# Second-layer dense tiles and mu products placed in the slots of layer 3's FFN tiles, last norms placed in the experts loop

## The chip, the cores and the metric

The kernel runs on one core of one Trainium2 chip. The metric is the device time in microseconds (us) of one execution. Three executions of the kernel before gave a median of 2058.72 us (2057.43 to 2061.12). Everything is float32.

The engines are TensorE (PE; PEld is its weight load), VectorE (DVE), ScalarE (ACT), GpSimd (POOL) and SyncE (SP, which only issues DMAs here). Each runs its own program in order and waits on semaphores for the others.

## The reference, cut to what matters

3125 nodes with 256 features, 53125 edges sorted by destination, in two halves with weights of their own.

```python
xn = _layernorm(x)
# graph part: two layers
h = xn + res * conv(xn, rel1, W_in1, W_out1, W_loop1, b1)
h = h  + res * conv(h,  rel2, W_in2, W_out2, W_loop2, b2)
g = h @ mu_w + mu_b
#   conv: m = x[src] * rel[type];  first half @ W_in, second half @ W_out
#         agg = segment_sum(m / deg[dst]);  tanh(agg + x @ W_loop + b)
# mix part: four layers (0 to 3) of linear attention and FFN on xn
x = x + g + mix(xn)
# last part: norm, gates over 4 experts (softmax, top 2, softmax again),
# shared MLP 256-256-128-256, experts 256-128-64-256
y = _layernorm(x);  x = x + shared(y) + sum(topw * expert(y))
```

## The kernel before, in words

Rows are worked on in 25 tiles (NT) of 125 nodes (T), five groups (NG) of five tiles (GT). The mix part runs layer by layer; a layer is a `joint` (end of attention's context) and five `iteration`s, one per group. In an iteration each tile's FFN is an up product (`Feed.up`, L2398: 16 matmuls of 125 columns in two halves), ScalarE's gelu, and a down product (`Feed.down`, L2413: 8 matmuls of 256 columns); beside them stand attention (`attend`) and turned rows (`turn`) of the next group. A float32 matmul is two instructions in the trace.

The graph layers run beside the mix layers as **edge steps** of 128 edges. GpSimd gathers a step's source rows (L837) and, in the first graph layer, its relation rows (L817). VectorE multiplies two steps at a time (a unit) with the relation rows and makes the one-hot rows of the destinations (`Edges.unit`, L959 and L968). TensorE sums them per destination (`Edges.unit` on TensorE, L2294), and VectorE adds every eight steps into `acc` (L947). The buffer holds 16 gathered steps, the one-hot ring 8. How many steps stand where is written out by hand (STEPS_GROUP, `marks`, and `upto(...)` between the FFN products); the same marks are used on VectorE and TensorE. The second graph layer has 416 steps: 92 in group 4 of layer 2, 36 in the joint of layer 3, and 60, 60, 60, 60, 48 in the groups of layer 3.

Once all steps of a graph layer are summed, the **dense** part takes each tile: VectorE scales the sums (L1483), TensorE turns sums and rows (L499) and multiplies them with the two weights (L2711), VectorE adds the bias (L1556), ScalarE takes the tanh (L2161), VectorE adds it to the rows (L1534). For the first graph layer this stands before group 4 of layer 2, for the second one (`dense(1)`) it stands behind all of layer 3. `dense_and_last` adds to the second one, some steps behind each tile, the mu product (`mu_beside`, L2782), its addition to the rows (`z_sum`, L1586, with the statistics in L1588), the last norm per group of five tiles (L1665 and `inv_sqrt`, then L1675), the turned norm rows and the gate logits (L2798, L1574). One piece more than tiles is needed because one tile holds edges of both halves. Gates are computed for 15 tiles at once and then for 10 (GATES). `general` is a path for unsorted edges, taken only if a flag made in the prologue is set; it stands behind the last edge step of each graph layer.

Last comes the **experts loop**: per tile `shared_1` (L2748), `turn_experts`, `experts_1` (L2757), `layer_2` (L2865, L2870) and `layer_3` (L2888, L2890) on TensorE, and `gated_rows` (L1828, L1831), `add_experts` (L1845) and `add_biases` (L1836, L1839) on VectorE. GpSimd adds x into the rows by DMA (`add_x`, L805) and loads the last weights (L874 to L888).

Of the kernel before, what the change touches and what calls it, by code (L numbers as in the profile page):

```python
# [14 lines left out]
P = 128  # L15
# [28 lines left out]
def build(nc, io, out):  # L44
# [37 lines left out]
    PD_INDICES, PD_ROWS, PD_FALLS, PD_KEYS = 3, 10, 21, 43  # L82
# [7 lines left out]
    LAST_LOADS = 11 + NX  # L90

# [9 lines left out]
    with ExitStack() as ctx:  # L101
# [98 lines left out]
        norm = qm[:, 0:NT]  # L200
# [36 lines left out]
        split_node_i, split_node = scratch(T, 1).bitcast(I32), scratch(T, 1)  # L237
# [5 lines left out]
        first, tile_of, base, place, bad = (scratch(SCH, 4) for _ in range(5))  # L243
# [16 lines left out]
        g_columns = hot[:, 1:1 + KC, :].rearrange("p s t -> p (s t)")  # L260
# [3 lines left out]
        gateb = key_tab[0:T, 0:NX]  # L264
        lmask = key_tab[0:T, NX:NX + NX * NX].rearrange("p (a b) -> p a b", b=NX)
# [12 lines left out]
        beat, beat2 = (last_buf(NT, NX, NX) for _ in range(2))  # L278
        assert last_at[0] <= GT * (D + AW)
        sb1p, sb2p, eb1p = b1p[:, 0:KC], b1p[:, KC:KC + 1], b1p[:, KC + 1:KC + 1 + NX]  # L280
# [248 lines left out]
        H2, MU, ZT = 2, 3, 11  # L529
        LG = ZT + 1  # L530
        DRAIN = LG + 2

# [3 lines left out]
        def dense_and_last(tile, beside):  # L536
            for t in range(NT + DRAIN):
                if t < NT:
                    tile(t)
                beside(t)  # L540

        def piece(g, t):

            return g * NB + t + 1


        GATES = (slice(0, 3 * GT), slice(3 * GT, NT))

        GATE_STEPS = (3, 4, 6)

        ps_logit = [ps_seg[1]] * 3 + [ps_kv, ps_dn]
        assert NG == len(ps_logit)
# [44 lines left out]
        for name, cols in (("mu", KC * D), ("sW1", KC * D), ("sW2", KC * P), ("sW3", D), ("eW1", NX * KC * P),  # L597
                           ("eW2", NX * EH2), ("eW3", KC * D), ("gW", KC * NX)):
            offs[name] = (at, at + cols)
            at += cols  # L600
        assert at <= 2 * KC * FF

        def last_w(name, c):
            a, b = offs[name]
            return wff[:, a:b].rearrange("p (c n) -> p c n", c=c)

        mu_w, sW1, sW2, gW = (last_w(n, KC) for n in ("mu", "sW1", "sW2", "gW"))
# [88 lines left out]
        def _(sp):  # L696
# [9 lines left out]
            sp.dma_start(split_node_i, io["dst"][HALF - 1:HALF].partition_broadcast(T)).then_inc(s_split, 16)  # L706
            load_ln1(sp, 0)

            def dense_rows(g):
# [19 lines left out]
                for t in range((NT - AHEAD) // AHEAD * AHEAD, NT):  # L729
                    if g == 0:  # L730
                        store_h1(t, t)
# [2190 lines left out]
```

## Time and profile before

| what | value |
|---|---|
| median of 3 executions | 2058.72 us |
| profiled execution | 2060.31 us |
| its span in the trace | 2058.6 us |
| TensorE busy | 1880.9 us (91%) |
| VectorE busy | 1259.6 us (61%) |
| ScalarE busy | 674.2 us (33%) |
| GpSimd busy | 1339.0 us (65%) |
| granted TensorE clock, mean | 0.979 |

The rows that follow are of three kinds. A row of a table of stretches gives busy time (and count) of each engine in a stretch. A row of a timeline gives the start of a run of like instructions, how long the run lasted, engine, line, operation, output and inputs, and in brackets how long the engine had been idle before it and what released it. The spacing of starts is the cadence of the engine, while the durations of overlapping matmuls add up to more. A row of groups gives busy time, mean duration of one and the idle time ahead of them. L-numbers are lines of the kernel before.

### The profile page before, as it was taken

The numbers are of one execution on the slowest core, as the hardware profiler recorded it, in microseconds if no ns is written. First come the engines' busy times: TensorE is split into PE (matmuls) and PEld (weight loads), VectorE is DVE, ScalarE is ACT, GpSimd is POOL, SyncE is SP. The second block draws the span as 40 slices with busy tenths as digits, with TensorE's granted clock in tenths as the row PEclk, the third lists the DMA queues.
The fourth block names the chain that finished last, engine by engine and source line by source line (L and its number), as shares of the span: only waits on it lengthen the run. The fifth ranks groups of instructions, "written<-read, shape, count | busy, mean of one in ns | idle before, by whom it ended". The sixth has DMA issues, their size and how long they took to land.

```text
span 2058.6 us, 32009 instructions
## 1 busy us (share of the span) xinstructions
PE 1880.9 (91%) x10496; PEld 1566.3 (76%) x10496; DVE 1259.6 (61%) x3295; ACT 674.2 (33%) x1858; POOL 1339.0 (65%) x1342
## 2 busy tenths in 40 slices
PE   3989999998999999989999897788988999899999
PEld 1558888886788888678888785566877778778998
DVE  6775576556657556665655654487656556456666
ACT  5432344343234334422433341122112112133443
POOL 5777777777777777777777227777777777720000
PEclk9999999999999999999999999899999999999999
DMA  8677666667766666776667337766666666650001
GB/s 240 186 247 217 199 188 193 204 198 239 229 197 190 196 202 197 239 227 196 192 205 215 94 114 262 222 200 213 199 192 201 194 199 198 148 106 14 14 16 36
DMA packets 191812, 371.61 MB, mean 181 GB/s; under 512 B 36589, under 2 KB 123035, under 8 KB 191656
## 3 DMA queue, kind: packets, MB, share of 16 engines
q0 software_dynamic: 78624, 225.58, 38.1%
q1 hardware_dynamic: 92986, 128.48, 19.1%
q10 hardware_dynamic: 20046, 15.57, 2.7%
q8 instruction: 86, 1.41, 0.3%
q14 instruction: 70, 0.57, 0.1%
HBM read 305.39 MB, written 64.95 MB: 180 GB/s over the span
## 4 chain that ended last, share of the span: by engine, by line
PE 58%; POOL 16%; DVE 10%; issue 7%; DMA 6%; ACT 2%; DVEq 1%; ACTq 0%; SPq 0%
POOL xg L837 13%; PE ps_down L2417 11%; PE ps_hid L2408 10%; PE ps_seg L2294 10%; PE ps_kv L2327 4%; DMA xg<-h_rows,idx_tab 4%; POOL rg L817 3%; PE ps_x L2372 2%; PE ps_hid L2757 2%; DVE xg L968 2%; PE ps_kv L2711 2%; PE ps_down L2711 2%; PE ps_x L499 2%; PE ps_hid L499 2%; PE ps_hid L2347 1%
## 5 line engine op out<-in xcount | busy, mean ns | idle before, releaser
L2294 PE MATMUL ps_seg<-xg,hot 128*125 128x257 f32 x1664 | 444.4, 395 | 85.6 <-DVE xg L968 84.8
L837 POOL DMA_INDIRECT xg<-h_rows,idx_tab x416 | 431.9, 1038 | 134.3 <-issue 116.4
L837 POOL DMA_INDIRECT xg<-xn_rows,idx_tab x416 | 431.3, 1037 | 127.8 <-issue 121.9
L817 POOL DMA_INDIRECT rg<-relation_rows,idx_tab x416 | 425.4, 1023 | 129.5 <-issue 129.2
L2294 PEld LDWEIGHTS ps_seg<-xg,hot 128*125 128x125 f32 x1664 | 293.9, 191 | 161.9 <-DVE xg L968 87.6
L2408 PEld LDWEIGHTS ps_hid<-hT,wff 128*128 128x128 f32 x3200 | 384.1, 192 | 15.8 <-issue 6.8
L2408 PE MATMUL ps_hid<-hT,wff 128*128 128x125 f32 x3200 | 387.9, 275 | 1.6 <-ACT gT L1950 0.9
L968 DVE TENSOR_TENSOR xg<-xg,rg 128x512 f32<-128x512 f32 x416 | 286.0, 688 | 157.2 <-DMA xg<-h_rows,idx_tab 129.5
L1950 ACT ACTIVATE gT<-ps_hid,b1p 128x125 f32<-128x125 f32 x800 | 225.9, 366 | 471.0 <-PE ps_hid L2408 470.8
L2417 PE MATMUL ps_down<-wff,gT 128*125 128x256 f32 x1600 | 368.0, 384 | 0.0
L2417 PEld LDWEIGHTS ps_down<-wff,gT 128*125 128x125 f32 x1600 | 299.7, 191 | 43.6
L959 DVE TENSOR_TENSOR hot<-iota_t,key_tab 128x250 f32<-128x250 f32 x416 | 170.9, 411 | 9.3 <-issue 5.3
L1134 DVE TENSOR_TENSOR xres<-xres,ps_down 125x256 f32<-125x256 f32 x100 | 40.1, 418 | 125.0 <-PE ps_down L2417 124.5
L2327 PE MATMUL ps_kv<-wqkv,hTa 128*125 128x512 f32 x240 | 113.7, 596 | 0.0
L1865 ACT ACTIVATE kx<-ps_kv 125x256 f32<-125x256 f32 x74 | 28.4, 384 | 249.3 <-PE ps_kv L2327 238.0
L1940 ACT ACTIVATE hT<-ps_x,ln2p 128x250 f32<-128x250 f32 (+1 forms) x120 | 56.0, 522 | 158.9 <-PE ps_x L499 158.5
L947 DVE SCALAR_TENSOR_TENSOR acc<-ps_seg,in_tile,acc 125x257 f32 x208 | 99.6, 479 | 4.2 <-PE ps_seg L2294 3.6
L1086 DVE TENSOR_TENSOR xres<-xres,ps_x 125x256 f32<-125x256 f32 x80 | 30.8, 418 | 113.3 <-PE ps_x L2372 113.3
L2372 PE MATMUL ps_x<-cwo,qT_all 128*125 128x256 f32 x320 | 77.7, 382 | 0.0
L2327 PEld LDWEIGHTS ps_kv<-wqkv,hTa 128*125 128x125 f32 x240 | 45.2, 189 | 33.8 <-issue 29.4
L2372 PEld LDWEIGHTS ps_x<-cwo,qT_all 128*125 128x125 f32 x320 | 60.4, 189 | 9.6
L1894 ACT ACTIVATE hTa<-ps_x,ln1p 128x125 f32<-128x125 f32 x120 | 48.3, 462 | 42.2 <-PE ps_x L499 42.2
(362 smaller groups left out, 2391.4 us busy)
## 6 DMA issues: line engine op xcount, KB each, us to landing
second_relation_rows<-rg SPq DMA_DIRECT2D x104, 512.0 KB, 4.0
rg<-second_relation_rows SPq DMA_DIRECT2D x104, 512.0 KB, 3.9
wff<-L_mix_W ACTq DMA_DIRECT2D x8, 1024.0 KB, 7.0
rg<-relation_rows,idx_tab POOLq DMA_INDIRECT x416, 3.5
xg<-xn_rows,idx_tab POOLq DMA_INDIRECT x416, 3.3
xg<-h_rows,idx_tab POOLq DMA_INDIRECT x416, 3.7
h_rows<-rg SPq DMA_DIRECT2D x25, 112.0 KB
xres<-x POOLq DMA_DIRECT2D x5, 560.0 KB, 8.6
```

Of the source, the lines that this page charges most:

```text
L499: ins = pe.transpose(dst[:, c * T:(c + 1) * T], rows[:, c * P:(c + 1) * P], ident[0:T, 0:T])
L817: pool.indirect_dma_start(rg[:, k, :], None, rel_d, bass.IndirectOffsetOnAxis(ap=idx_tab[:, step, 1:2], axis=0))\
L837: pool.indirect_dma_start(xg[:, k, 0:D], None, rows, bass.IndirectOffsetOnAxis(ap=idx_tab[:, step, 0:1], axis=0))\
L947: dve.scalar_tensor_tensor(a, ps_seg[w % 2][0:T, 0:AW], in_tile[:, ds(w, 1), m], a, ALU.mult, ALU.add).then_inc(s_acc, 1)
L959: dve.tensor_tensor(hot[:, hs:hs + UNIT, :], iota_t[:, :].unsqueeze(1).broadcast_to([EP, UNIT, T]), key_tab[:, at:at + UNIT].unsqueeze(2). ...
L968: dve.tensor_tensor(m, m, r, ALU.mult).then_inc(s_msg, 1)
L1950: ins = act.activation(gT[:, j % 2, ff, :], ps_hid[hf][:, f * T:(f + 1) * T], ACT.Gelu, bias=b1p[:, ff:ff + 1])
L2294: ins = pe.matmul(ps_seg[u // UW % 2][0:T, 0:AW], hot[:, s % HOTS, :], xg[:, s % RING, :], start=s % WIN == 0, stop=s % WIN == WIN - 1)
L2327: ins = pe.matmul(ps_kv[0:T, :], hTa[:, j % 2, c, :], wqkv[:, c, 0:2 * D], start=c == 0, stop=c == KC - 1)
L2372: ins = pe.matmul(ps_b[j % 2][0:T, :], q[:, c * T:(c + 1) * T], cwo[:, c, :], start=c == 0, stop=c == KC - 1)
L2408: ins = pe.matmul(ps_hid[hf][:, f * T:(f + 1) * T], w1[:, c, ff * P:(ff + 1) * P], hT[:, j, c, :], start=c == 0, stop=c == KC - 1)
L2417: ins = pe.matmul(ps_down[j % 2][0:T, :], gT[:, j % 2, f, :], w2[:, f, :], start=f == 0, stop=f == FC - 1)
```

## The change

The second graph layer's dense tiles no longer wait for the last edge. Destinations are sorted, so a tile's sums are complete once the edge windows that reach it are added (`windows_of`). A piece k of the 26 (25 tiles and the split tile's extra product as piece 11) is carried through two slots, and an iteration of layer 3 has ten slots between its FFN products: `aside(0)` to `aside(9)`. Rows of the first layer's result come tile by tile over ScalarE's DMA queue into `qrow`. The mu products follow two pieces later. What is left of pieces 24 and 25 stands behind the last group.

The last norm of group 0 is made in the last iteration, those of groups 1 to 4 in the experts loop (tile by tile of the loop: statistics and norm; rows; turned rows; logits; gates). Gates are made for five tiles at a time. The branch to the general path of the second layer moves ahead of layer 3's groups; its flag is also set if an edge comes earlier than the new order allows, or if the split lies outside tiles 11 to 13. Loads of the last weights move from GpSimd's to SyncE's queue. GpSimd's adds of x wait for the group's mu sums too. Nothing changes in the numbers of edge steps and their marks.

```diff
 # VectorE
-            def iteration(lay, gi, upto, one, early, sums_done, joint_rest):
+            def iteration(lay, gi, upto, one, early, sums_done, joint_rest, aside):
...
                 upto(m["up0"])
+                if not is_first(gi):
+                    aside(-1)
...
                 upto(m["up1"])
+                aside(0)
                 upto(m["down0"])
+                aside(1)
                 b.add_ffn(0)
...
                 early()
+                aside(8)
+                if (lay, gi) == (L - 1, NG - 1):
+                    last_norm(0)
                 b.add_ffn(3)
...
+            def dense_beside(s):
+                k = s // 2
+                if s % 2 == 0:
+                    rows_updated(k - 1)
+                    mu_added(k - 2)
+                    sums_scaled(k + 1)
                 else:
-                    dense_and_last(dense_tile, lambda t: z_beside(t, update))
+                    product_biased(k)
...
+                    if (lay, gi) == (L - 1, 0):
+                        general(1)
+                        self_split.read()
+                        sums_scaled(0)
+                        gate_order()
...
-            dense(1)
+            behind = NG * (2 * GT)
+            dense_beside(behind - 1)
+            dense_beside(behind)
+            logits(0)
+            shift_logits(0)
+            dense_beside(behind + 1)
+            dense_beside(behind + 2)
+            softmax(0)
+            top_two(0)
+            dense_beside(behind + 4)
+            gates(0)
...
             for s in range(1, NT + 2):
+                gi, j = last_part(s)
                 if s <= NT:
                     gated_rows(s - 1)
                 if s > 1:
                     add_experts(s - 2)
                 if s <= NT:
                     add_biases(s - 1)
-                if s in GATE_STEPS:
-                    gate_steps[GATE_STEPS.index(s) + 1](1)
+                if gi < NG:
+                    if j == 0:
+                        last_stats(gi)
+                    if j == 1:
+                        last_rows(gi)
+                    if j == 3:
+                        logits(gi)
+                        shift_logits(gi)
+                    if j == 4:
+                        softmax(gi)
+                        top_two(gi)
+                        gates(gi)
 # ScalarE
+            def dense_beside(s):
+                k = s // 2
+                if s % 2 == 0:
+                    loop_tanhs(k - 1)
+                    sums_turned(k)
+                else:
+                    rows_turned(k - 1)
...
                 b.gelu(0)
+                aside(0)
                 b.gelu(1)
...
+                aside(1)
+                aside(2)
...
+                aside(3)
+                aside(4)
                 b.gelu(3)
...
+                aside(5)
+                aside(6)
                 b.gelu(4)
+                aside(7)
 # TensorE
                 up(0, None)
+                aside(0)
                 up(1, "up0")
...
+                aside(1)
                 b.down(0)
...
                     n.attend(1)
+                aside(2)
...
+                aside(3)
...
                 b.down(1)
                 upto(m["down1"])
+                aside(4)
...
+                aside(5)
...
                 b.down(2)
                 upto(m["down2"])
+                aside(6)
                 up(4, "down2")
+                aside(7)
...
                 b.down(3)
                 upto(m["down3"])
+                aside(8)
...
                 b.down(4)
                 upto(m["ctx"])
+                aside(9)
...
+            def dense_beside(s, split_tile):
+                k = s // 2
+                if s % 2 == 0:
+                    turn_sums(k)
+                    mu_product(k - 2)
                 else:
-                    dense_and_last(dense_tile, mu_beside)
+                    sum_product(k, split_tile)
+                    turn_rows(k - 1)
...
+            behind = NG * (2 * GT)
+            turn_last(0)
+            turn_last(1)
+            dense_beside(behind, split_tile)
+            for j in range(2, GT):
+                turn_last(j)
+            dense_beside(behind + 1, split_tile)
+            last_logits(0)
+            pe.wait_ge(s_ew, 16 * LAST_LOADS)
+            pe.wait_ge(s_gel, L * (2 * NT) + 2)
+            shared_1(0)
+            dense_beside(behind + 2, split_tile)
+            experts_1(0)
+            dense_beside(behind + 3, split_tile)
+            dense_beside(behind + 4, split_tile)
             for s in range(1, NT + 2):
...
                 if s < NT:
                     shared_1(s)
+                if gi < NG and j == 3:
+                    last_logits(gi)
+                turn(0)
                 if s > 1:
                     turn_experts(s - 2)
+                turn(1)
 # GpSimd
             def add_x(gi):
                 pool.wait_ge(s_xr, NG * L + gi + 1)
+                pool.wait_ge(s_emz, (gi + 1) * GT)
...
+                    if g == GL - 1 and step == at_group[L - 1, 0] - STEPS2:
+                        hold(pool, s_seg, g * UNITS + step // UNIT + 1)
+                        general(1)
```

## Rows read from the trace of the kernel before

**Rows 1.** table of stretches: us from to, length, busy (count) per engine, clock, DMA share, GB/s
```profile
1415.00:1495.00 80.00, 72.29 (x394) 62.08 (x393) 49.92 (x128) 15.61 (x47) 62.33 (x59) 0.96 0.63 200
...
1797.00:1916.00 119.00, 106.93 (x630) 92.53 (x629) 70.14 (x250) 43.91 (x110) 16.00 (x21) 0.94 0.28 58
...
1916.00:2058.00 142.00, 138.01 (x1079) 132.66 (x1079) 95.08 (x228) 55.69 (x196) 0.00 (x0) 0.99 0.08 24
```

**Rows 2.** the page's groups: the gathers of the second graph layer
```profile
L837 POOL DMA_INDIRECT xg<-h_rows,idx_tab x416 | 431.9, 1038 | 134.3 <-issue 116.4
```

**Rows 3.** who waited for whom, TensorE, 1415 to 1797 us: total, times, longest
```profile
PE ps_seg L2294 <- DVE xg L968: 34.9, 46, 3.1
```

**Rows 4.** timeline of TensorE, layer 3, group 0 and the last down product
```profile
1415.40 1.94 PE L2408 MATMUL ps_hid<-hT,wff 128*128 128x125 f32 x16
...
1472.03 3.62 PE L2417 MATMUL ps_down<-wff,gT 128*125 128x256 f32 x16
1475.48 1.03 PE L2294 MATMUL ps_seg<-xg,hot 128*125 128x257 f32 x4
1476.35 1.94 PE L2408 MATMUL ps_hid<-hT,wff 128*128 128x125 f32 x16
1478.13 1.90 PE L2294 MATMUL ps_seg<-xg,hot 128*125 128x257 f32 x8
...
1495.50 1.95 PE L2408 MATMUL ps_hid<-hT,wff 128*128 128x125 f32 x16
...
1793.49 3.62 PE L2417 MATMUL ps_down<-wff,gT 128*125 128x256 f32 x16
```

**Rows 5.** timeline of TensorE, dense tiles and logits behind layer 3
```profile
1819.26 0.38 PE L499 MATMUL ps_hid<-ident,xg 125*128 125x125 f32 x2
...
1819.69 1.89 PE L2711 MATMUL ps_kv<-wqkv,gT 128*125 x8
1821.42 0.38 PE L499 MATMUL ps_x<-ident,acc 125*128 125x125 f32 x2
1821.64 1.03 PE L2782 MATMUL ps_seg<-wff,hT 128*125 128x256 f32 x4
1822.50 0.38 PE L499 MATMUL ps_hid<-ident,xg 125*128 125x125 f32 x2
...
1850.08 0.50 PE L2798 MATMUL ps_seg<-wff,qT_all 128*125 128x4 f32 x4
```

**Rows 6.** timeline of VectorE, experts loop: gated rows and experts added
```profile
1965.48 0.42 DVE L1828 TENSOR_TENSOR xh<-ps_x,bo_b 125x256 f32<-125x256 f32 x1 [1.32 <-PE ps_x L2870]
...
1966.83 0.42 DVE L1845 TENSOR_TENSOR xres<-xres,ps_kv 125x256 f32<-125x256 f32 x1 [0.47 <-PE ps_kv L2890]
```

**Rows 7.** timeline of ScalarE behind layer 3; table loads from 1797 us on
```profile
1812.43 0.42 ACT L2161 ACTIVATE acc<-acc 125x256 f32<-125x256 f32 x1 [2.78 <-DVE acc L1556]
...
L2210 ACT ACT_TABLE_LOAD x1 | 1.3, 1283 | 0.0
```

**Rows 8.** timeline of VectorE in the prologue: the first multiplied messages
```profile
51.08 0.69 DVE L968 TENSOR_TENSOR xg<-xg,rg 128x512 f32<-128x512 f32 x1 [3.59 <-DMA xg<-xn_rows,idx_tab]
```

**Rows 9.** timeline of TensorE, experts loop: starts of the shared product
```profile
1916.38 2.05 PE L2748 MATMUL ps_hid<-qT_all,wff 128*128 128x125 f32 x8
...
1961.05 1.05 PE L2748 MATMUL ps_hid<-qT_all,wff 128*128 128x125 f32 x8
...
1966.56 1.05 PE L2748 MATMUL ps_hid<-qT_all,wff 128*128 128x125 f32 x8
```

**Rows 10.** timeline of VectorE: last norm of five tiles, gates of 15 tiles
```profile
1905.65 0.45 DVE L1665 BATCH_NORM_AGGREGATE mv<-stat 125x2 f32<-125x6 f32 x5
...
1908.15 1.70 DVE L1675 TENSOR_SCALAR acc<-xres,mv,rstd 125x256 f32<-125x256 f32 x5
...
1914.39 0.22 DVE L1607 TENSOR_REDUCE kx<-kx 125x15 f32<-125x60 f32 x1 [4.16 <-ACT kx L2210]
...
1918.94 0.18 DVE L1574 TENSOR_TENSOR kx<-ps_kv,key_tab 125x20 f32<-125x20 f32 x1
```

More of the change, by code:

```diff
@@ L90, in build, with due_node, windows_of, tile_of_piece @@
     LAST_LOADS = 11 + NX
+    REST = 11
+    SPLITS = range(REST, REST + 3)
+    DUE_STEP, DUE_NODE, DUE_PITCH = 51 * WIN, (NT - 1) * T + 4, 125.0 / 2048.0
+    def due_node(edge):
+        return DUE_NODE + (edge - DUE_STEP * EP) * DUE_PITCH
+    def windows_of(t):
+        for w in range(STEPS2 // WIN):
+            chunk, step = divmod(w * WIN, SCH)
+            if due_node(CHUNKS[chunk][0] + step * EP) >= (t + 1) * T:
+                return w
+        return STEPS2 // WIN
+    def tile_of_piece(k):
+        return k if k < REST else -1 if k == REST else k - 1
+    def has_tile(k):
+        return 0 <= k < NB and k != REST
     xn_d = nc.dram_tensor("xn_rows", [N, D], F32, kind="Internal").ap()
@@ L242, in build @@
         spans = scratch(SCH, 4 * EP).rearrange("p (c t) -> p c t", c=4)
-        first, tile_of, base, place, bad = (scratch(SCH, 4) for _ in range(5))
+        first, tile_of, base, place, bad, due = (scratch(SCH, 4) for _ in range(6))
         reached = scratch(SCH, 4 * (NT - 1)).rearrange("p (c t) -> p c t", c=4)
@@ L1438, in general @@
             def general(g):
[L1440 removed]
+                row, other, onehot, turned = G_ROWS[g]
+                ps_turned, ps_product, ps_summed = ps_general[g]
+                if g == 0:
+                    hold(dve, s_acc, 2 * WINS + 3)
+                else:
+                    hold(dve, s_cw, L)
                 with dve.If(dve.value_load(unsorted_i[0:1, 0:1], min_val=0, max_val=1) == 1):
@@ new lines, in dense, with sums_scaled @@
+                update(NT - 1)
+                hold(dve, s_hn, NT)
+                dve.wait_ge(s_azero, NB)
+            def sums_scaled(k):
+                if not 0 <= k < NB:
+                    return
+                t = tile_of_piece(k)
+                need = windows_of(SPLITS[-1] if t < 0 else t)
+                assert edges.added() >= need, (k, edges.added(), need)
+                dve.wait_ge(s_acc, WINS * 2 + edges.adds + 3)
+                edges.scaled += 1
+                if k > 1:
+                    dve.wait_ge(s_dtr, SLOTS + NB + k - 1)
+                at, factor = (self_split.rest, norm[:, ds(self_split.rest_norm, 1)]) if t < 0 else                     (self_split.tile_sums(t), norm[:, t:t + 1])
+                dve.tensor_scalar(sums2[k % 2], at_tile(acc, at)[:, 0:D], factor, None, ALU.mult).then_inc(s_sc, 1)
@@ L1732, in _ @@
             p(dve.tensor_reduce(bad, spans, AX, ALU.add))
+            p(dve.tensor_tensor(due, due, first, ALU.is_gt))
+            p.wait()
+            p(dve.tensor_tensor(bad, bad, due, ALU.add))
             p.wait()
```

742 lines of the change are left out of this document (423 added, 319 removed).

## The prediction

> **What bounds the kernel now.** I read the table of stretches first [rows 1]. In the first group of layer 3 all engines work together: TensorE is shown busy 72.3 of 80 us, GpSimd 62.3, VectorE 49.9, ScalarE 15.6, and the same pattern holds for the next three groups. From 1797 us on GpSimd has nothing more to gather, and TensorE alone sets the pace: 119 us up to the experts loop, then 142 us of that loop. So 261 of 2058.6 us run with GpSimd idle and, before them, TensorE shares its time with a gather stream that it often waits for.
>
> Who waits for whom in layer 3 comes second. GpSimd issues one gather per edge step: 1038 ns busy and 134.3/416 = 0.32 us before each, nearly all of it put down to issue, not to a wait [rows 2]. A step therefore costs 1.36 us, a group of 60 steps 81.7 us, and the group measured 1495.50 - 1415.40 = 80.1 us [rows 4]. TensorE waits 34.9 us for multiplied messages, in 46 pieces [rows 3]; nothing else holds it there. Layer 3 is gather-bound.
>
> What TensorE really needs I take from starts, not from durations, since matmuls overlap [rows 4]. The down product of a tile takes 1475.48 - 1472.03 = 3.45 us, two edge steps 0.87 (0.435 each), half an up product 1.78 (3.56 per tile). The attention product of a tile is two matmuls of 256 columns like those of mu, 0.86, and a pair of transposes 0.22 [rows 5]. A tile is 8.1 us, five are 40.5, 60 steps are 26.1: 66.6 us of work in an 80 us group. The last group (48 steps, no next group to attend) needs 35.1 + 20.9 = 56.0. Together 322 us of work lie between 1415.40 and the end of the last down product at 1793.49 + 3.5 = 1797 us, 381.6 us. TensorE has 59 us of holes there.
>
> **The change part by part.**
>
> *Dense tiles and mu move into layer 3.* A tile of the second layer's dense work is, start to start, 1822.50 - 1819.26 = 3.24 us of TensorE: sums and rows turned 0.43, four matmuls 1.73, the new rows turned 0.22, mu 0.86 [rows 5]. Over five groups the 50 slots hold 24 tiles' turns and products (24 x 2.16 = 51.8), the split tile's extra product (1.1), 23 turns back (5.0) and 22 mu products (18.9): 76.8 us. TensorE's need becomes 322 + 76.8 = 399 us against 381.6 measured, so the bound changes hands: an inner group asks 66.6 + 15.4 = 82 us of TensorE, 80 to 82 of GpSimd. Two streams that are this close don't fill every hole; I add 6 us for holes that stay (1 to 2 us a group instead of 13.6). The lower end is 17 us (TensorE never waits), the upper is 77 (no hole used); I take 17 + 6 = 23, since 34.9 us of waits are scattered over 46 places and the slots come every 8 us. VectorE gets about 1.6 us more per tile (scale, bias, update, mu added, 0.35 to 0.48 each by like operations [rows 6]), 8 us a group on top of 46 to 50 of 80: covered. ScalarE gets two copies and a tanh, some 1.3 us a tile on top of 15.6 us a group: covered. Which waits are late next: the product needs ScalarE's copy from one slot earlier, and a 3.5 to 7 us FFN product lies between; the turn back needs VectorE's update, issued just after the same edge units that TensorE has yet to multiply, with 1.7 us of the sum product ahead of it. I cost these at nothing; the rival below prices them.
>
> *Tanh among gelus.* The row shows Tanh in the tail, after layer 3's gelus, with no table load between, and the only load after 1797 us is that of the gates' Exp, 1283 ns [rows 7]. So nothing is added. The Trainium skill ("ScalarE: Activation LUTs", section on table sets) lists tanh with exp and with sigmoid, gelu as the anchor of a set of its own, and advises batching by set; by that rule each tile would switch twice. The trace disagrees with that reading, but it is a rival below.
>
> *General path and index work ahead of layer 3.* It isn't taken: the destinations are sorted and the new due condition adds nothing to the count for these inputs (the closest edge lies 119 nodes above its bound, from the input arrays). What remains is a value load and a branch on three engines, four memsets and a read of the split numbers on VectorE, ahead of group 0, and a branch inside GpSimd's gather stream, which delays every later gather. No row shows it alone. Ends 0 and 8 us; I take 3. The dozen small VectorE operations in the prologue (under 0.2 us each, 2 us) hide behind the first gather, for which VectorE sat idle 3.59 us [rows 8]: 0.
>
> *Loads.* The last weights go from GpSimd's queue to SyncE's and start some 20 steps before the end, mu's weights and the h1 rows to ScalarE's. They land long before their readers; the experts' first tile has more than 20 us. The adds of x still follow the last gather and land while the last edges are summed. Nothing. Earlier loads could slow the last gathers: under 3 us, in the range.
>
> *The drain.* Before, 1916.38 - 1793.49 = 122.9 us pass from the last edge product (the last down product starts there) to the loop's first shared product [rows 4, 9]. After, what is left there, from that same point: VectorE's last adds and slot 8, 2.8; norm of group 0: statistics 1.8 and then 1908.15 - 1905.65 = 2.5 [rows 10]; first row 0.4: 7.8 (TensorE's down product and tile 24's products run beside it). Two FFN adds, bias of tile 24, mu of tile 23: 11.5. Turned rows, tile 25's product: 14.4. Five pairs of logits at 0.4 (0.50 shown for one [rows 5]): 16.4. Shared product, mu, experts' product: 20.4. ScalarE's relus and the copy for the last mu product, which TensorE waits for: 23.8. So 24 us, ends 20 and 34, and 99 us are saved.
>
> *The experts loop.* It runs at 1966.56 - 1961.05 = 5.51 us a tile on TensorE, with VectorE idle 1.32 and 0.46 us [rows 6, 9]: slack 1.78 a tile. New per group of five tiles on TensorE: 5 x (0.22 + 0.36) = 2.9. New on VectorE: 4.3 (statistics, norm) in one tile, 1.7 (rows) in the next, 0.6 and 3.6 (gates; 1918.94 - 1914.39 = 4.55 for 15 tiles, less for 5) later [rows 10]. The 3.6 and the next group's 4.3 stand in tiles that follow each other: 7.9 + 1.7 against 3 x 1.78 of slack and 1.05 us by which the gated rows were early leave TensorE waiting 3.3. So 6.2 a group, four groups: 25 us. The ends are 12 (VectorE wholly hidden) and 40 (all 10.2 us of VectorE in series).
>
> *Sum.* 23 + 3 - 99 + 25 = -48 us. The profiled execution took 2060.31 us (span 2058.6 and 1.7 around it), so 2012.3; it lay 1.6 above the median of 2058.72, so 2010.7. I forecast 2011.
>
> **The rivals.**
> 1. *Hand-over stalls* (the slower side): each slot puts TensorE in order behind a step of ScalarE or VectorE. If VectorE stands at a wait of its own when its part is due (it waits for gathers and for FFN products there now), TensorE idles and the gathers with it. Over 50 slots it decides from 48/50 = 0.96 us each; at 1.2 us the time is 2011 + 60 = 2071. For it: VectorE's idle share. Against it: the slots of the three programs stand behind the same edge marks. 0.06. At 0.5 us each it is 2036: 0.12.
> 2. *The loop hides VectorE's work*: 12 in place of 25, 1998. The gates and rows are short and TensorE's own extra work gives VectorE time. 0.17.
> 3. *The loop takes it in series*: 40 in place of 25, 2026. 0.12.
> 4. *Table loads*: 24 tiles x 2 x 1283 ns [rows 7] = 62 us, on the path 2073; against it stands the tanh row. 0.01. The skill page's rule named above is this mechanism; its own figure with the drain (2.66 us) would make it estimated at 128 us.
> 5. *Taken general path*, or the order of the slots not as the text says: 0.01, far slower.
>
> **How the numbers follow.** Forecast 0.51. The range must take in rivals 2 and 3 and the layer term's spread: the low end is 2011 - 13 (rival 2) - 6 (no holes left) - 2 = 1990; the high end 2011 + 25 (half-microsecond stalls) + 4 = 2040. A measurement here can tell about 0.2%, 4 us. Faster 0.90, within 0.2% 0.03 (the far flank of rival 1), slower 0.07.
>
> **What would show it.** Right: groups of layer 3 at 82 to 85 us with TensorE's waits for messages below 15 us; last edge product at 1815 to 1825; 22 to 30 us to the loop; loop tiles of 5.5 us with one stop of 2 to 4 us in five, before the turn of gated rows. Wrong: groups at 90 us with waits for ScalarE's copies or VectorE's updates (rival 1); a table load per tile (4); the last edge still at 1795 (TensorE's need overrated); loop tiles even at 6.1 (2) or at 7.5 (3).

## The result

| | changed kernel | kernel before |
|---|---|---|
| median of 15 runs, us | 2050.37 (2043.79 to 2054.97) | 2063.2 (2057.43 to 2076.59) |
| ratio, 95% interval | 0.9927 (0.9912 to 0.9942) | |
| profiled execution, us | 2053.1 (span 2051.4) | 2060.31 (span 2058.6) |

The change makes the kernel faster by 0.73% (0.58 to 0.88%), about 13 to 15 us. The forecast was 48 us less, 2011, with a range that ended at 2040: right in the sign, wrong in the size, and the measured 2050.37 lies outside the range. In the comparisons below, a run that took over 1.5% more than the fastest run of its kernel is left out.

The table of stretches of the changed kernel: us from to, length, busy us (instructions) of PE, PEld, DVE, ACT and POOL, granted clock as a share of full speed, DMA share, GB/s. The first five are the groups of layer 3, the sixth is the drain, the last the experts loop.

```profile
1424.00:1504.00 80.00, 74.08 (x423) 65.69 (x424) 53.20 (x143) 19.55 (x56) 61.71 (x61) 0.98 0.71 217
1504.00:1591.00 87.00, 85.00 (x483) 75.98 (x483) 52.60 (x132) 20.76 (x62) 64.12 (x60) 0.98 0.61 187
1591.00:1677.00 86.00, 85.74 (x496) 76.38 (x495) 52.49 (x133) 21.16 (x62) 63.60 (x62) 1.00 0.63 193
1677.00:1764.00 87.00, 85.00 (x483) 75.84 (x482) 52.24 (x131) 20.87 (x62) 67.57 (x62) 0.98 0.61 191
1764.00:1838.00 74.00, 74.00 (x438) 66.45 (x437) 39.32 (x94) 18.95 (x57) 46.55 (x44) 1.00 0.70 165
1838.00:1857.00 19.00, 15.11 (x98) 12.90 (x97) 9.66 (x43) 7.33 (x20) 0.00 (x0) 1.00 0.01 1
1857.00:2051.00 194.00, 164.08 (x1195) 155.05 (x1194) 122.65 (x377) 63.62 (x222) 2.30 (x2) 0.91 0.08 21
```

Against [rows 1]: in layer 3 TensorE has few holes left (5.9 us in the first group, 0 to 2.0 in the others), and the 119 us between the last gather and the loop are 19. But the loop, 142 us at a clock of 0.99 before, is 194 us at 0.91, with TensorE idle for 30 of them. The same in the waits of TensorE (us in total, times, longest), layer 3 first, then the experts loop:

```profile
PE ps_seg L2469 <- DVE xg L1008: 3.8, 2, 2.7
PE ps_kv L2985 <- DVE zeros L1644: 3.8, 2, 2.0
PE ps_kv L2985 <- DVE kx L1644: 2.0, 1, 2.0
PE ps_hid L2583 <- issue: 0.8, 1, 0.8
...
PE ps_seg L528 <- DVE acc L1690: 19.4, 4, 4.9
PE ps_down L3134 <- issue: 3.5, 5, 0.9
PE ps_kv L3134 <- issue: 2.6, 4, 0.9
PE ps_seg L528 <- DVE xh L1940: 1.1, 1, 1.1
```

The 34.9 us for messages [rows 3] have become 3.8. New are three stops of up to 2.0 us ahead of mu's product (L2985), for VectorE's bias of the dense product (L1644), and in the loop four stops of 4.7 to 4.9 us ahead of a turn (L528), for VectorE's norm rows (L1690).

The marks that the sum is made of, on TensorE's timeline (start us, us, engine, line, operation): the first up product of layer 3, its last down product, the loop's first shared product, the last product of all.

```profile
1424.41 2.02 PE L2583 MATMUL ps_hid<-hT,wff 128*128 128x125 f32 x16 [0.83 <-issue]
...
1834.95 3.62 PE L2592 MATMUL ps_down<-wff,gT 128*125 128x256 f32 x16
...
1856.72 1.05 PE L3027 MATMUL ps_hid<-qT_all,rg 128*128 128x125 f32 x8
...
2047.51 1.03 PE L3136 MATMUL ps_down<-rg,hTa 128*125 128x256 f32 x4
```

| stretch, us | before | changed | difference | forecast |
|---|---|---|---|---|
| to layer 3's first up product | 1415.4 | 1424.4 | +9.0 | (within the 3 for the branch) |
| from there to the last down product | 378.1 | 410.5 | +32.4 | +26 with the branch |
| to the loop's first shared product | 122.9 | 21.8 | -101.1 | -99 |
| to the last product (2054.72 before) | 138.3 | 190.8 | +52.4 | +25 |
| to the end | 3.9 | 3.9 | 0 | 0 |

In sum -7.3, which is the difference of the two spans. The medians lie further apart (12.8) because the profiled execution of the changed kernel was 2.7 us above its median and that of before 2.9 us below its own. Against the forecast the profiles miss 41 us (the medians 35): 27 in the loop, 9 ahead of layer 3, 6 in it, and 2 the other way in the drain. The question for the experiments is the loop.

This is a part of its first group on TensorE, from the third shared product to the fifth.

```profile
1866.58 1.05 PE L3027 MATMUL ps_hid<-qT_all,rg 128*128 128x125 f32 x8
1872.33 0.68 PE L528 MATMUL ps_seg<-ident,acc 125*128 125x125 f32 x2 [4.70 <-DVE acc L1690]
1872.81 0.62 PE L528 MATMUL ps_seg<-ident,xh 125*128 125x125 f32 x2
1873.58 0.65 PE L528 MATMUL ps_seg<-ident,acc 125*128 125x125 f32 x2
1874.02 3.34 PE L3036 MATMUL ps_hid<-qT_all,rg 128*128 128x125 f32 x16
...
1880.70 1.06 PE L3027 MATMUL ps_hid<-qT_all,rg 128*128 128x125 f32 x8
1881.59 2.25 PE L3015 MATMUL ps_seg<-rg,qT_all 128*125 128x4 f32 x20
...
1883.94 1.95 PE L3036 MATMUL ps_hid<-qT_all,rg 128*128 128x125 f32 x16
...
1888.35 1.05 PE L3027 MATMUL ps_hid<-qT_all,rg 128*128 128x125 f32 x8
```

One tile takes 14.1 us (1866.58 to 1880.70), the next 7.65, where 5.51 is a tile's pace [rows 9]. Two things stand in the first: a stop of 4.70 us, and behind it an experts' product of 3.34 us that takes 1.95 in the next tile: the 1.2 GHz level of the clock for as long as the records are longer. Behind all four stops this product takes 3.2 to 3.6 us, and in the second and fourth group the clock falls once more a tile later, with no stop directly ahead (3.28 us at 1924.35, 3.40 at 2006.40). VectorE at the time of the first stop, from the gated rows (L1937, L1940) that the turn behind it needs:

```profile
1868.33 0.42 DVE L1937 TENSOR_TENSOR xh<-ps_x,bo_b 125x256 f32<-125x256 f32 x1
1868.78 0.42 DVE L1940 SCALAR_TENSOR_TENSOR xh<-xh,kx 125x256 f32<-125x256 f32 x1
1869.12 0.41 DVE L1954 TENSOR_TENSOR xres<-xres,ps_down 125x256 f32<-125x256 f32 x1
1869.45 0.42 DVE L1945 TENSOR_TENSOR xres<-xres,b_b 125x256 f32<-125x256 f32 x1
1869.91 2.05 DVE L1948 SCALAR_TENSOR_TENSOR xres<-kx,xres 125x256 f32<-125x256 f32 x4
1871.87 1.70 DVE L1690 TENSOR_SCALAR acc<-xres,mv,rstd 125x256 f32<-125x256 f32 x5
1878.95 0.42 DVE L1937 TENSOR_TENSOR xh<-ps_x,bo_b 125x256 f32<-125x256 f32 x1 [5.38 <-PE ps_x L3114]
```

The gated rows that TensorE needs for this tile were ready at 1869.2. What it waited for was the first norm row of the *next* group, 3 us later, because that turn stands in its order ahead of the turn of the gated rows and of the experts' product. And then VectorE, thought to be the engine in short supply, sat idle for 5.38 us.

### The profile page after: what moved, and what is told of

It is laid out like the page before. It is cut to its first block, busy times and chain, and to the rows that moved or that the text cites. A ratio compares the mean times of both kernels' runs of the same rounds, so it can differ in the third digit from the quotient of the medians.

```text
span 2051.4 us, 32102 instructions
## 1 busy us (share of the span) xinstructions
PE 1881.3 (92%) x10496; PEld 1580.4 (77%) x10496; DVE 1260.1 (61%) x3348; ACT 677.7 (33%) x1864; POOL 1336.9 (65%) x1324
## 4 chain that ended last, share of the span: by engine, by line
PE 63%; POOL 15%; DVE 11%; issue 7%; DMA 2%; ACT 1%; DVEq 1%; SPq 0%; ACTq 0%
PE ps_seg L2469 13%; PE ps_hid L2583 12%; PE ps_down L2592 12%; POOL xg L906 9%; POOL rg L862 6%; PE ps_kv L2502 3%; PE ps_kv L2891 3%; PE ps_x L2547 3%; PE ps_x L528 2%; PE ps_hid L3036 2%; DVE xg L1008 1%; DVE xres L1948 1%; PE ps_hid L2522 1%; PE ps_kv L2985 1%; PE ps_down L2891 1%
## 5 line engine op out<-in xcount | busy, mean ns | idle before, releaser
L906 POOL DMA_INDIRECT xg<-h_rows,idx_tab x416 | 439.0, 1055 | 148.5 <-issue 117.4
L862 POOL DMA_INDIRECT rg<-relation_rows,idx_tab x416 | 433.4, 1042 | 128.9 <-issue 128.6
L906 POOL DMA_INDIRECT xg<-xn_rows,idx_tab x416 | 426.9, 1026 | 128.2 <-issue 123.4
L2469 PE MATMUL ps_seg<-xg,hot 128*125 128x257 f32 x1664 | 436.4, 395 | 54.3 <-DVE xg L1008 53.8
L2469 PEld LDWEIGHTS ps_seg<-xg,hot 128*125 128x125 f32 x1664 | 300.8, 193 | 114.7 <-DVE xg L1008 49.3
L999 DVE TENSOR_TENSOR hot<-iota_t,key_tab 128x250 f32<-128x250 f32 x416 | 170.7, 410 | 10.7 <-issue 5.2
```

The lines of the kernel that those rows point to most:

```text
L862: pool.indirect_dma_start(rg[:, k, :], None, rel_d, bass.IndirectOffsetOnAxis(ap=idx_tab[:, step, 1:2], axis=0))\
L906: pool.indirect_dma_start(xg[:, k, 0:D], None, rows, bass.IndirectOffsetOnAxis(ap=idx_tab[:, step, 0:1], axis=0))\
L999: dve.tensor_tensor(hot[:, hs:hs + UNIT, :], iota_t[:, :].unsqueeze(1).broadcast_to([EP, UNIT, T]), key_tab[:, at:at + UNIT].unsqueeze(2). ...
L2469: ins = pe.matmul(ps_seg[u // UW % 2][0:T, 0:AW], hot[:, s % HOTS, :], xg[:, s % RING, :], start=s % WIN == 0, stop=s % WIN == WIN - 1)
```

## The experiments

Theory A: the loop is long because of the order in which the new work stands, not because of how much it is; TensorE waits at the first turn, and each such stop also costs time at half clock. Theory B: VectorE's work of 10.2 us a group does not fit into five tiles, and any order ends in the same stop somewhere else. For layer 3: TensorE sets its pace now, so its three stops count in full (A), or the gathers take over right behind (B).

The code cuts below are shortened: they show the moved calls and leave the rest out. The experiments ran on other chips than the result. There the kernel before takes 2381 to 2411 us in place of 2063, and the changed kernel 0.9976 (0.9938 to 1.0013) of it, so that the gain of the result does not show there. What is longer lies in the gather stages: in the changed kernel's profile there GpSimd waits 262.5 us for ring slots,

```profile
POOL xg L906 <- PE ps_seg L2469: 262.5, 93, 15.9
```

and 27.2 in the profile of the result. Many waits there (285.5 us of ScalarE's ahead of the gelus among them) are put down to a releaser outside the profile, so the profiles do not show why. The experts loop has no gathers, and its length agrees across these chips (190.8 us in the result's profile, 190.1 to 190.7 in four profiles there whose loop is that of the changed kernel), so the loop is compared by its own length, from the first shared product (s = 1) to the last product. Layer 3 can only be compared roughly.

### Norms ahead of the loop again

```diff
-                    if j == 0: last_stats(gi)
-                    if j == 1: last_rows(gi)
-                    if j == 3: logits(gi); shift_logits(gi)
-                    if j == 4: softmax(gi); top_two(gi); gates(gi)
+            for gi in range(1, NG):          # ahead of the loop, VectorE
+                last_norm(gi); logits(gi); shift_logits(gi)
+                softmax(gi); top_two(gi); gates(gi)
```

and the turns, logits and exponentials of the other two engines with them.

> The last norms, turns, logits and gates of groups 1 to 4 are taken out of the experts loop again and done one group after the other ahead of it; the dense tiles stay in layer 3. Theory A (the loop's 12.4 to 14.5 us more per group are the interleaved norm and gate work with its stop and the half clock behind it): the loop goes back to 138 to 142 us, the drain grows by four chains in series of about 11 us each (norm 5.9, turns and logits 1.3, gates 4), 44 us: 5 to 10 us faster than the changed kernel or equal to it, the interleaving earned nothing. Rival B (the loop is slower for another reason of the change, such as where its weights now lie): the loop stays at 170 us or more and the time is 30 to 44 us above the changed kernel.

Measured: 2436.61 us, 1.0101 (1.0047 to 1.0155) of the kernel before. The loop takes 2427.08 - 2288.87 = 138.2 us, that of the kernel before to 0.1 us. So nothing else of the change (the weights in the ring of relation rows, the turned rows in other places) slows it: all 52.4 us are the interleaved work with what it drags behind. My price for the four chains in series was too low by far, 74 us against 44:

```profile
2259.17 0.68 PE L528 MATMUL ps_seg<-ident,acc 125*128 125x125 f32 x2 [9.01 <-DVE acc L1690]
...
2265.25 4.33 PE L3012 MATMUL ps_seg<-rg,qT_all 128*125 128x4 f32 x20 [0.56 <-ACT qT_all L1979]
2278.59 0.68 PE L528 MATMUL ps_seg<-ident,acc 125*128 125x125 f32 x2 [9.00 <-DVE acc L1690]
```

A chain is 19.4 us (2259.17 to 2278.59), with TensorE at the lower level of its clock throughout (granted 0.51 from 2215 to 2289): five turns 1.21 to 1.24 us apart, the last three waiting for ScalarE's copies, and logits of 4.2 us that take 2.1 at full clock. The interleaving was right as an idea: it took 75 us out of the drain (97.7 from the last down product to the loop here, 22.9 in the changed kernel on such a chip) and put 52 into the loop.

### TensorE's order alone

```diff
                 shared_1(s)
-                if j == 3: last_logits(gi)
-                turn(0)              # all five in tile j == 2
-                turn_experts(s - 2); turn(1)
-                experts_1(s); turn(2)
-                layer_2(s - 1); turn(3)
-                layer_3(s - 2); turn(4)
+                if j == 3: turn(3)
+                turn_experts(s - 2)
+                if j == 3: turn(4)
+                experts_1(s)
+                if j == 2: turn(0)
+                if j == 3: last_logits(gi)
+                layer_2(s - 1)
+                if j == 2: turn(1)
+                layer_3(s - 2)
+                if j == 2: turn(2)
```

ScalarE's copies stand accordingly.

> TensorE's (and ScalarE's) order alone: in the experts loop the turn of the next group's first norm row stands behind the turn of the gated rows and behind the experts' product, the other four turns follow one by one to the next tile. Theory A (the order makes the stop: VectorE's norm rows come late and everything else of TensorE stands behind the first turn): the one stop of 4.7 to 4.9 us a group becomes one of about 1.7 (gated rows ready at 1869.2, TensorE free at 1867.5) and one of about 1, four groups save 8 to 12 us; where the clock no longer falls behind the shorter stop, another 1.5 to 3 a group, down to 20 less in all. Loop 171 to 183 us instead of 190.8. Rival B (VectorE's work itself is the limit of these tiles, the stop only moves): within 3 us of the changed kernel, the same idle time in front of the turn of the gated rows.

Measured: loop 2396.7 - 2219.0 = 177.7 us, 13 less, with VectorE's program untouched. The time, 0.9927 (0.9888 to 0.9965), has no run of the changed kernel on the same chip beside it.

```profile
PE ps_seg L528 <- DVE xh L1940: 7.4, 4, 1.9
...
PE ps_seg L528 <- ACT qT_all L1984: 2.8, 4, 0.7
PE ps_seg L528 <- DVE acc L1690: 2.4, 3, 0.8
```

The stop of 4.7 is one of 1.7 to 1.9 for the gated rows, as worked out from the row of 1869.2, and in three of four groups one of 0.8 for the norm row. The experts' product behind the stop of 1.7 to 1.9 takes 1.95 us in three groups and 3.58 in one.

### VectorE's order alone

```diff
+                if gi < NG and j == 1:
+                    last_rows(gi)
                 if s <= NT:
                     add_biases(s - 1)
-                    if j == 1:
-                        last_rows(gi)
```

> VectorE's order alone: in the experts loop the five norm rows of the next group stand ahead of the expert biases of the same tile instead of behind them. The first row is then ready 2.5 us earlier. Theory A: stop 4.8 -> 2.3 us, four groups save 10 us, and 14 to 16 if the clock falls less behind it. Rival B (VectorE's load is the limit): the biases delay the gated rows of the next tile and TensorE waits there instead, within 3 us of the changed kernel.

Measured: loop 2377.6 - 2197.1 = 180.5 us, 10.3 less; 0.9889 (0.9837 to 0.9941) of the kernel before. The waits for norm rows are 10.7 us in place of 19.4, the longest 2.5. The clock still falls behind all four shorter stops: the experts' product there takes 3.2 to 3.6 us. No wait for gated rows appeared in their place, which is what theory B asked for. Two programs, each with one order changed and no operation removed, and each takes 10 to 13 us out of the loop: the limit wasn't the amount of work.

### Work in the stop

The products are unused; the two waits keep them off results that are still read, and the row of 2207.00 below shows no idle time for them.

```diff
                 turn(0) of tile j == 2:
+                    pe.wait_ge(s_exT, gi * GT)
+                    pe.wait_ge(s_elr, gi)
+                    for k in range(20):
+                        pe.matmul(ps_seg[1][:, 0:T], sW1[:, k % KC, 0:P], columns_of(s)[:, k % KC, :],
+                                  start=True, stop=True)
                     turn_last(gi * GT)
```

> The changed kernel with 20 unused products of 128 by 125 (40 matmuls of 0.11 us, 4.4 us) put into the stop of TensorE ahead of each first turn in the experts loop; nothing else changes and their results are overwritten. Theory A (the half clock behind the stop is caused by the stop and costs 1.4 us in the first experts' product, about 1 in the turns and up to 1.3 in the next product): loop 180 to 185 us instead of 190.8, the products behind the former stop at 1.95 us, not 3.2 to 3.6. Rival B (the clock falls there for another reason): loop 190 us or more, the products stay at 3.3 us.

Measured: loop 2377.52 - 2196.26 = 181.3 us, 9.5 less than in the result's profile (8.9 to 9.5 less than in the four on such chips), although TensorE has four times 4.6 us more to do. The time, 0.9937 (0.9902 to 0.9972), has no run of the changed kernel on the same chip beside it.

```profile
2207.00 4.63 PE L3164 MATMUL ps_seg<-qT_all,rg 128*128 128x125 f32 x40
2211.86 0.43 PE L528 MATMUL ps_seg<-ident,acc 125*128 125x125 f32 x2 [0.22 <-DVE acc L1690]
...
2213.09 1.95 PE L3036 MATMUL ps_hid<-qT_all,rg 128*128 128x125 f32 x16
```

The experts' product behind the former stop takes 1.95 us in all four groups, not 3.2 to 3.6, and of the two later falls one is left, in another group (2.83 us). The fall of the clock is a consequence of the stop, and its price is now a measured one: some 9.5 us in four groups, 2.4 for each stop of 4.8.

### The work spread over the tiles

Rows in tile 1, the next group's statistics in tile 2, logits and softmax in tile 3, gates in tile 4, the next group's root in tile 5; group 1's statistics in a wait of the drain. VectorE's part, the other engines accordingly:

```diff
+                if gi < NG and j == 0: last_rows(gi)
+                if gi < NG and j == 2: logits(gi); shift_logits(gi)
                 if s <= NT: add_biases(s - 1)
+                if gi < NG and j == 2: softmax(gi)
+                if gi < NG and j == 3: top_two(gi); gates(gi)
+                if gi + 1 < NG and j == 1: last_moments(gi + 1)   # statistics
+                if gi + 1 < NG and j == 4: last_root(gi + 1)      # reciprocal root
```

> All three engines' orders of the norm and gate work in the experts loop: group 1's statistics move into VectorE's idle 4.97 us ahead of the first logits, then in each group of five tiles rows in tile 1, the next group's statistics in tile 2, logits and softmax in tile 3, gates in tile 4, the next group's root in tile 5; turns in tiles 2 and 3. The same operations, at most 2.6 us of them on VectorE per tile (slack there 1.78 a tile and 1.05 early). Theory A (only the order made the loop long): no stop over 1 us, loop 138.3 + 4 x 2.9 + about 3 of small waits = 150 to 156 us instead of 190.8, 35 to 40 us less than the changed kernel. Rival B (VectorE's 10.2 us a group do not fit whatever the order, or the clock stays down): loop at 165 us or more.

Measured: loop 2331.8 - 2176.8 = 155.0 us, 35.2 less than in the changed kernel on the same chip (190.2). Three more profiles of this loop, in the studies of both orders below, show 155.0, 156.6 and 153.3. The time is 2348.16 beside 2382.0 of the changed kernel, 34 us less; against the kernel before 0.9852 (0.9797 to 0.9908) beside 0.9976.

```profile
PE ps_seg L528 <- DVE xh L1948: 1.1, 1, 1.1
PE ps_down L3146 <- issue: 0.6, 1, 0.6
```

These are all the waits of TensorE in the loop, and both lie in its last tile. Group 1's statistics (4 us of VectorE) now stand ahead of the loop; all else is the same operations on the same engines, and groups 2 to 4 have all of theirs in the loop without a stop: theory B is gone.

### The bias ahead of the root in layer 3

```diff
-                    n.stats(lambda: one(m["up4"] - 1))
+                    n.stats(between)     # its second call, behind the aggregates, does aside(5)
                 upto(m["down2"])
-                aside(5)
+                if not n: aside(5)
```

> Layer 3 alone: in groups with a next group to attend, VectorE adds the product's bias of slot 5 right behind the aggregated statistics of the attention norm, ahead of the ten steps of its reciprocal root, instead of behind them. Theory A: the stops of 1.75 to 2.0 us that TensorE makes in front of mu's product in slot 6 go, and with them the half clock that follows (an up product half of 3.34 in place of 1.95 us at 1577): 2.0 + 1.6 us in three to four groups, 8 to 14 us less. Rival B (GpSimd's stream of gathers, 1.36 us a step and 81.7 a group, takes over as the bound): 5 us less at most, with waits for messages coming back. Rival C: nothing, since the norm rows behind the root are late instead.

Measured 0.9946 (0.9914 to 0.9978). A second study of the same kernel:

> The early bias of slot 5 alone, as before, wanted on a chip where the kernel before takes some 2060 us and layer 3 is not held by its gathers. Theory A (TensorE sets layer 3's pace, each stop of 2.0 us in slot 6 costs another 1.6 of half clock): 8 to 14 us less than the changed kernel's 0.9927 of the kernel before, that is 0.986 to 0.989; inner groups at 82.5 to 83.5 us. Rival B (gathers take over at 81.7 a group): 0.990 to 0.993. Where the kernel before takes 2390 us or more, about 0.995 and no verdict.

Measured 0.9938 (0.9907 to 0.9969) beside 2393.96 us of the kernel before, so this is the case without a verdict. With the spread order on top:

> The spread order of the loop with the early bias of slot 5 in layer 3 as well. Theory A (TensorE sets layer 3's pace): 8 to 14 us less than with the spread order alone, inner groups 82.5 to 83.5 us instead of 86.6, no wait of TensorE for the bias in slot 6. Rival B (gathers take over): 5 us less at most. On a chip where the gathers take longer than in the profile of the kernel before, Rival B holds and says nothing about the other.

Measured 2336.98 us, 11 less than the spread order alone on the same chip; 0.9788 (0.9744 to 0.9832). Twice more, on two other chips:

> Spread order of the loop and early bias together, wanted on a chip where the kernel before takes some 2060 us. Theory A: 35 us (loop) and 8 to 14 us (layer 3) less than the changed kernel, 2000 to 2007 where that takes 2050, ratio 0.970 to 0.975. Rival B (the loop's gain is taken back by the clock, or layer 3's by the gathers): 0.977 to 0.982. Where the kernel before takes 2390 us or more: about 0.979, as in the first such run.

> Both orders again. Theory A: where the kernel before takes some 2060 us, 2000 to 2007, inner groups of layer 3 at 82.5 to 83.5 us from the last down product of one to the last of the next, no stop in slot 6, loop 155. Rival B: groups at 85 to 86 us all the same, 2012 or more. Where the kernel before takes 2390 us, 0.977 to 0.979 of it.

Measured 0.9766 (0.9721 to 0.9811) and 0.9766 (0.9685 to 0.9847). The stops themselves are gone: the changed kernel on such a chip waits 2.8, 2.0 and 1.7 us ahead of mu's product in layer 3, the five profiles with the early bias never over 1.0. From the first to the last down product of layer 3 these five show 427.6, 428.0, 434.8, 436.2 and 436.2 us, mean 432.6; the six with the old order and all of its work 438.2, 439.6, 440.7, 442.0, 447.1 and 452.4, mean 443.3. That is 11 us less, of the size of theory A, and on both chips that have profiles of either kind the early bias has the shorter ones (436.2 against 442.0 to 452.4, and 427.6 against 438.2 and 439.6). But profiles of one layer 3 program on one chip lie 8 to 10 us apart, the intervals of the two kernels on one chip overlap, and on none of these chips is layer 3 free of other waits. It is likely, not settled.

### Half of mu's product

```diff
-                for c in range(KC):
-                    ins = pe.matmul(ps_kv[0:T, D:2 * D], hTa[:, t % 2, c, :], mu_w[:, c, :], ...)
+                ins = pe.matmul(ps_kv[0:T, D:2 * D], hTa[:, t % 2, 0, :], mu_w[:, 0, :], start=True, stop=True)
```

> The changed kernel with one of the two matmuls of each mu product left out (half of the contraction is missing, so that the sums are not the reference's): 0.43 us of TensorE in each of 25 tiles, 22 of them in layer 3. Theory A (TensorE sets layer 3's pace): 22 x 0.43 = 9.5 us less in layer 3. Rival B (layer 3 is still paced by gathers or by hand-overs): under 3 us.

Measured 2379.1 us, 0.9964 (0.9915 to 1.0013) of the kernel before. The changed kernel on the same chip:

> The changed kernel itself beside the others on their chip: 0.9927 of the kernel before where gathers land in 3.4 us; from 0.99 to 1.00 where they take longer, since layer 3 then has room for the dense tiles but the experts loop loses the same 52 us.

Measured 2382.0 us, 0.9976 (0.9938 to 1.0013). The 9.5 us of theory A are 0.4% and lie within these intervals, so the times tell A from B no better than the profiles: there the stretch between the first and the last down product is 7.9 us shorter (431.7 and 439.6), of the size of A, but other profiles of one program lie as far apart. With these chips' waits it can't be said whether layer 3 would give the 9.5 us back where it is held by nothing else.

## Why the prediction failed

**What bounds the kernel.** Right. Layer 3 was gather-bound with 59 us of holes, and the dense tiles changed that: waits for messages fell from 34.9 to 3.8 us (below 15 was forecast).

**The drain.** Right to 2 us: 23.8 forecast, 21.8 measured, 101 us saved. The chain was added up from [rows 4, 5, 9, 10] and came out in the order written, each step 1 to 2 us early (first norm row turned after 5.9 us, forecast 7.8, whose terms add up to 7.5; logits done after 15.0, forecast 16.4).

**Tanh among gelus.** Right. 23 tanhs stand between gelus in layer 3, and the one table load of the stretch is the first gelu's own:

```profile
L2242 ACT ACTIVATE zeros<-zeros 125x256 f32<-125x256 f32 x12 | 5.0, 418 | 15.5 <-DVE zeros L1644 15.4
L2242 ACT ACTIVATE kx<-kx 125x256 f32<-125x256 f32 x11 | 4.6, 418 | 18.5 <-DVE kx L1644 18.5
L2069 ACT ACT_TABLE_LOAD x1 | 1.3, 1283 | 4.8 <-PE ps_hid L2583 4.8
```

Rival 4 is gone. The Trainium skill ("ScalarE: Activation LUTs", section on table sets) would have a switch at each of them; the trace doesn't agree.

**Layer 3.** The mechanism was right, one size was off. TensorE's need was put at 399 us, to the end of the last down product. The same stretch is 410.5 + 3.5 = 414.0 us long; less 10.7 us of waits it is 403.3, of which some 5 are half clock, as added up from the longer records. So the need was right to a few us. On top I expected 6 us of holes and found 10.7 us of waits and those 5 of half clock, for which there was no term, and I had costed the hand-overs at nothing. Three of them cost 5.8 us, and twice the clock fell behind them:

```profile
1490.88 1.10 PE L2985 MATMUL ps_kv<-wo,hTa 128*125 128x256 f32 x4 [1.75 <-DVE zeros L1644]
...
1575.88 1.39 PE L2985 MATMUL ps_kv<-wo,hTa 128*125 128x256 f32 x4 [2.00 <-DVE kx L1644]
1577.06 3.34 PE L2583 MATMUL ps_hid<-hT,wff 128*128 128x125 f32 x16
...
1743.65 1.90 PE L2985 MATMUL ps_kv<-wo,hTa 128*125 128x256 f32 x4 [2.00 <-DVE zeros L1644]
1745.34 2.85 PE L2583 MATMUL ps_hid<-hT,wff 128*128 128x125 f32 x16
```

The engine named is right and the reason is plain in the code: VectorE issues the bias of slot 5 behind the norm's root, ten short dependent steps of 0.2 us, although the product is ready before them. This is rival 1 in 3 of 50 slots: 5.8 us, far from the point from which it decides. I had looked at what each slot waits for on the other engine, and not at what stands ahead of that operation in the other engine's order. Of the three inner groups two took 86.6 and 86.7 us where 82 to 85 stood, and the one between them 81.1. That one holds the split tile's extra piece, so that no mu product falls due at this place and TensorE does not stop: of the 5.5 us between them some 3.8 are the stop of 2.0 and the half clock behind it, by the starts around 1575.88, and 1.7 a mu product and half a sum product less (0.86 each).

**The way to layer 3.** 3 us were taken for the branch. TensorE's wait that belongs to it is 0.83 us (the first mark above). That the wait is the branch's is read off its place, not shown apart. The other 8 us came before: 7 in one place at 660 to 680 us, which the change doesn't touch,

```profile
669.45 2.05 PE L2469 MATMUL ps_seg<-xg,hot 128*125 128x257 f32 x4 [3.36 <-DVE xg L1008]
```

a late gather and half clock behind it, absent in the profile of before. VectorE waits 4.48 us there for a gather of relation rows. It looks like the chance of one execution, in line with where the two profiled executions lie by their medians; no run here shows it apart.

**The experts loop: the step that failed.** "3 x 1.78 of slack and 1.05 us by which the gated rows were early leave TensorE waiting 3.3", and with 2.9 us for the turns and logits 6.2 a group. (Added up again, the amounts give 3.2, not 3.3; that changes nothing.) It measured 13.1 a group, 52.4 in all, beyond the end of 40 that I had given for VectorE wholly in series. Two errors are in that sentence.
1. It is a balance of amounts. I let TensorE wait only where it needs the gated rows and took the turns as work that adds 0.22 us each. But a turn is also a wait, and the first stands ahead of the rest of its tile. The order was in the diff; I did not lay VectorE's operations and TensorE's side by side. The stops are 4.85 us each, and VectorE idles 5.4 us right behind: it waits for TensorE, which has waited for it. By this, "all in series" was no upper end either.
2. It has no term for the clock. The loop ran at 0.99 before, and I kept that level for a loop with a stop in each group. The filled stop shows the price: 9.5 us.

The runs split the 52.4 us: 9.5 are half clock behind the stops (filled stop), 26.3 more go with the order (181.3 - 155.0: stops of 19.4 us and small waits of 6), and 16.7 stay when nothing waits (155.0 - 138.3; 15 to 18 over the four profiles of the spread loop), against 11.6 by my count of turns and logits. The small waits are the same error on a third engine. The profile calls them "issue", but ScalarE's copy that TensorE's product reads ends 0.1 us before it, and the copy stands in ScalarE's order behind an exponential that waited for VectorE's logits:

```profile
1892.00 0.22 ACT L2360 ACTIVATE kx<-kx 125x20 f32<-125x20 f32 x1 [4.68 <-DVE kx L1714]
...
1892.62 0.38 ACT L1984 ACTIVATE hTa<-ps_seg 128x250 f32<-128x250 f32 x1
...
1893.10 0.67 PE L3134 MATMUL ps_kv<-rg,gT 128*125 128x256 f32 x2 [0.42 <-issue]
```

With the good order the loop's term would have been 17, between my lower end of 12 and my 25. The forecast of 2011 was nearer to a well-ordered loop: by an estimate, the measured 2050.4 less the 35.8 us of the order and its half clock is 2015; no run on the chip of the result shows it. Rival 3 had the right sign of this, with a chance of 0.12 and a price that was 12 us too small.

The version with both orders mended takes 0.977 to 0.979 of the kernel before on the chips of the experiments, where the changed kernel takes 0.998 in its one study there: 45 us less side by side (2336.98 and 2382.0).

## What to carry to other kernels

When work is put between the steps of a tight loop, a balance of busy time gives only the lower bound. Write the two engines' orders next to each other and ask of each new instruction what it waits for, when that is ready, and what stands behind it in its queue; the cheapest place for a turn is behind the work it doesn't need, and work that only has to be ready tiles later can be cut into pieces of one tile's slack. And count a stop of TensorE at more than its length: the half clock behind it belongs to the term.

## What the hardware showed that I had not expected

- A stop of 4.8 us of TensorE costs another 2.4 us behind it (filled stop), part of it a tile later. Halving the stop does not halve that: behind stops of 2.3 to 2.5 us (VectorE's order alone) the product still took 3.2 to 3.6 us in place of 1.95. Shorter stops differ: behind 1.75 us at 1490.88 the next product ran at full clock, behind 2.00 us at 1575.88 an up product took 3.34 us, and behind four stops of 1.7 to 1.9 us (TensorE's order alone) three products took 1.95 us and one 3.58.
- Ten matmul calls of only 4 columns (logits of five tiles, 20 matmuls) take 2.1 us at full clock and 4.2 at half: 0.21 us a call, about what a matmul of 125 columns takes, too. Their price is the number of calls, not their columns.
- The same program took 2063 us on one chip and 2381 to 2411 on five others; the changed kernel's experts loop, which has no gathers, was the same to 1 us (190.1 to 190.8), the spread one to 3 us (153.3 to 156.6). What makes the other stages longer there stays open.
